# A decoder layer in one launch: the last self-attention batch reordered, and the last two routed tiles given other buffers

## The reference

```
x = layernorm(x + self_attention(x))      # 16 heads of 64, w_qkv 256x3072, w_out 1024x256, bias
x = layernorm(x + cross_attention(x, ctx))# 16 heads of 16, 375 keys, mask, four 256x256 weights
x = layernorm(x + moe(x))                 # top-1 of 8 experts (silu(gate)*up, down; hidden 512) + shared expert
```

## Time and profile before

| | us |
|---|---|
| median of 3 runs (lowest, highest) | 426.57 (425.27, 428.22) |
| the profiled execution's own time | 427.74 |
| its span | 426.0 |
| mean granted TensorE clock, share of full | 0.988 |

### The profile page before, as it was taken

One profiled execution on the slowest core, in us unless ns is written; L12 is line 12 of the kernel. 1 busy time (PEld: TensorE's weight loads), 2 busy tenths in 40 slices (PEclk: granted clock), 3 DMA queues, 4 the chain that ended last, 5 costly groups with the idle time before them and its releaser, 6 DMA issues.

```text
span 426.0 us, 13100 instructions
## 1 busy us (share of the span) xinstructions
PE 400.1 (94%) x5166; PEld 299.7 (70%) x5167; DVE 253.0 (59%) x729; ACT 208.4 (49%) x603; POOL 50.9 (12%) x79
## 2 busy tenths in 40 slices
PE   8999999999999788999999999999899999999980
PEld 7867877878777565766666666666565476899970
DVE  1367775856757555666667676768673641254432
ACT  1064463343625526687666666667683104344420
POOL 4010000101011001000001010100100054223223
PEclk9999999999999899999999999999999999999996
DMA  8999000000000014050404040920000013222211
GB/s 265 367 382 270 14 2 3 3 4 2 4 3 2 4 38 148 2 187 2 187 0 185 16 171 2 390 95 2 0 4 2 2 62 100 62 62 70 61 34 34
DMA packets 15257, 34.49 MB, mean 81 GB/s; under 512 B 2382, under 2 KB 9151, under 8 KB 13921
## 3 DMA queue, kind: packets, MB, share of 16 engines
q1 hardware_dynamic: 13952, 30.72, 20.5%
q0 software_dynamic: 1104, 2.76, 1.8%
q10 hardware_dynamic: 144, 0.23, 0.2%
HBM read 27.27 MB, written 6.70 MB: 80 GB/s over the span
## 4 chain that ended last, share of the span: by engine, by line
PE 42%; issue 38%; DVE 9%; POOL 3%; ACT 3%; DMA 3%; POOLq 1%; SPq 0%; DVEq 0%; ACTq 0%
PE banks L445 9%; PE banks L831 5%; PE banks L467 4%; PE banks L522 3%; PE banks L487 3%; PE banks L509 3%; PE banks L902 3%; PE banks L923 2%; PE banks L843 2%; DVE p L1159 2%; ACT p L977 2%; PE banks L912 2%; DMA out_x<-p,ids 2%; DVE pT L1168 1%; DVE nm L1151 1%
## 5 line engine op out<-in xcount | busy, mean ns | idle before, releaser
L1289 DVE CUSTOM_DVE_ANT_0 p<-banks,mask 112x375 f32<-112x375 f32 x128 | 62.6, 543 | 28.2 <-PE banks L634 28.1
L1031 ACT ACTIVATE p<-p,nm 112x375 f32<-112x375 f32 x128 | 73.8, 604 | 5.3 <-DVE nm L1289 5.3
L1038 ACT ACTIVATE pT<-banks 128x336 f32<-128x336 f32 x96 | 42.4, 443 | 42.1 <-PE banks L654 41.8
L977 ACT ACTIVATE p<-banks,nm 128x112 f32<-128x112 f32 x128 | 43.4, 365 | 31.7 <-DVE nm L1151 30.5
L654 PEld LDWEIGHTS banks<-ident,p 112*128 112x128 f32 (+1 forms) x384 | 38.3, 139 | 28.9 <-issue 22.1
L654 PE MATMUL banks<-ident,p 112*128 112x112 f32 (+1 forms) x384 | 53.2, 266 | 2.0 <-DVE nm L1289 1.5
L445 PE MATMUL banks<-x2T,arena 128*128 128x224 f32 x256 | 52.1, 359 | 0.0
L445 PEld LDWEIGHTS banks<-x2T,arena 128*128 128x128 f32 x256 | 48.5, 193 | 1.8 <-ACT arena L967 0.2
L360 POOL TENSOR_TENSOR rstd<-veps,minus_half 128x1 f32<-128x1 f32 x14 | 7.7, 551 | 286.8 <-DVE veps L1183 286.8
L1144 DVE TENSOR_SCALAR arena<-banks 128x448 f32<-128x448 f32 x32 | 19.9, 621 | 28.5 <-PE banks L445 28.4
L467 PE MATMUL banks<-arena,x2T 128*32 128x256 f32 (+1 forms) x512 | 29.9, 381 | 0.9 <-issue 0.5
(11 more groups left out here) (143 smaller groups left out, 589.7 us busy)
## 6 DMA issues: line engine op xcount, KB each, us to landing
arena<-in_ug SPq DMA_DIRECT2D x8, 1024.0 KB, 5.5
arena<-in_dn SPq DMA_DIRECT2D x8, 512.0 KB, 6.4
mid<-in_ctxT SPq DMA_DIRECT2D x8, 375.0 KB, 3.0
slots_s<-blank SPq DMA_DIRECT2D x14, 128.5 KB
arena<-in_wqk SPq DMA_DIRECT2D x7, 256.0 KB, 5.9
slots_x<-blank SPq DMA_DIRECT2D x14, 128.0 KB
p<-slots_s SPq DMA_DIRECT2D x9, 128.5 KB, 2.1
kT<-slots_x SPq DMA_DIRECT2D x9, 128.0 KB, 2.0
```

The costliest lines, as they stand in the source:

```text
L977: e = act.activation(p1[g][:, i, 0:S], PE_S1[g % 2][:, i * 128:i * 128 + S], ACT.Exp, bias=nm1[:, n:n + 1], accum_out=rs1[:, n:n + 1])
L1031: act.activation(p2[i % RING], p2[i % RING], ACT.Exp, bias=nm2[:, i % H:i % H + 1], scale=-1.0).then_inc(exp2, 1)
L1038: act.activation(pT2[:, i % RING], PE_T2[r][:, 0:KT * S].rearrange("p (k n) -> p k n", k=KT), ACT.Copy).then_inc(pt2_act, 1)
L1289: v.tensor_tensor_reduce(p2[i % RING], PE_S2[r][0:S, 0:S2], bias[:], 1.0, 3e38, ALU.add, ALU.min, accum_out=nm2[:, i % H:i % H + 1]).then_ ...
```

## The change

In batch 7 (`OUT_EARLY`) TensorE issues `out1(5)` ahead of `score1(1,7)` instead of behind it, and `value1(0,7)` ahead of `between1(7,5)` (the second key half) instead of behind it. VectorE takes the residual sum of tile 5 (`add_rest`) and `evac_v(2,0)` right behind the last row maxima, `evac_q(0)` ahead of `normalise(3)` instead of behind it, and the moments behind `turn_blocks(3)`, with `ln1_b(5)` directly after them.

In the routed tiles the product of tile 8 goes to `hrT_last`, in the array `mid`, and no longer waits for `down(7)`. Tile 7 takes `ids[1]`, `fin[1]` and a semaphore of its own for its store; tile 8 takes `ids[0]`, `fin[0]` and waits for the stores of tiles 0 to 6. GpSimd's loop ends one tile earlier, the last two tiles are written out. SyncE's last wait is split in two.

```diff
+        OUT_EARLY = (B - 1,)
-            def to_out(t, p):
+            def to_out(t, p, done=stored):
...
-            with g.Fori(0, tiles - 1) as t:
+            with g.Fori(0, tiles - 2) as t:
                 root3(t, 0)
                 to_out(t, 0)
-            root3(tiles - 1, 1)
-            to_out(tiles - 1, 1)
+            root3(tiles - 2, 1)
+            to_out(tiles - 2, 1, stored_other)
+            root3(tiles - 1, 0)
+            to_out(tiles - 1, 0)
...
                 between1(b, 1)
+                if b in OUT_EARLY:
+                    out1(b - 2)
                 score1(1, b)
-                if b >= 2:
+                if b >= 2 and b not in OUT_EARLY:
                     out1(b - 2)
...
                 between1(b, 4)
-                between1(b, 5)
                 if b == B - 1:
                     value1(0, b)
-                if b < 2 or b == B - 1:
+                between1(b, 5)
+                if b < 2 or b in OUT_EARLY:
                     value1(1, b)
...
                 rowmax(3, b)
-                if b < 2:
+                if b in OUT_EARLY:
+                    add_rest(PE_W1[:, 0:C], wout1, xb1, b - 2, b % 2, y1)
+                if b < 2 or b in OUT_EARLY:
                     drain1(b, 0)
                 normalise(2, b)
                 turn_blocks(2, b)
-                if b >= 2:
+                if b >= 2 and b not in OUT_EARLY:
                     ln1_a(b - 2)
                     drain1(b, 0)
                 else:
                     drain1(b, 1)
                 normalise(3, b)
                 turn_blocks(3, b)
+                if b in OUT_EARLY:
+                    moments(b - 2, b % 2, y1, st1, ag1, ve1)
                 if b >= 2:
                     ln1_b(b - 2)
+                if b >= 2 and b not in OUT_EARLY:
                     drain1(b, 1)
...
-            def finish(t, first, p=0):
+            def finish(t, first, p=0, kept=0):
...
                 if not first and p == 0:
-                    v.wait_ge(stored, t * 16)
+                    v.wait_ge(stored, t * 16 - kept)
...
-            product(tiles - 1, False)
-            finish(tiles - 2, False)
-            finish(tiles - 1, False, 1)
+            product(tiles - 1, True, hrT_last)
+            finish(tiles - 2, False, 1)
+            finish(tiles - 1, False, 0, 16)
```

More of the change, by code:

```diff
@@ L177, in build @@
         lgT = mid[:, 0, 0:2 * TILE]
-        hr = mid[:, 0, 0:HID]
+        hrT_last = mid[:, 0, 0:HID].rearrange("p (k n) -> p k n", k=HT)
         hrT = spent[:, 2 * C:2 * C + HID].rearrange("p (k n) -> p k n", k=HT)
@@ L232, in build @@
             sem(n) for n in ("xst_pe", "xst_sb", "gu_pe", "g_sb", "h_sb", "wg_sb", "wu_sb", "yr_pe"))
-        sum3, ids_sb, stats3, aggr3, ve3s, rstd3, done3, stored = (
-            sem(n) for n in ("sum3", "ids_sb", "stats3", "aggr3", "ve3s", "rstd3", "done3", "stored"))
+        sum3, ids_sb, stats3, aggr3, ve3s, rstd3, done3, stored, stored_other = (
+            sem(n) for n in ("sum3", "ids_sb", "stats3", "aggr3", "ve3s", "rstd3", "done3", "stored", "stored_other"))
         PE_S1, PE_J1, PE_U1, PE_W1 = bank[0:2], bank[2:4], bank[4:8], bank[7][:, 256:512]
@@ L324, in _ @@
             load_shared(tiles - 1)
-            sp.wait_ge(stored, tiles * 16)
+            sp.wait_ge(stored, tiles * 16 - 16)
+            sp.wait_ge(stored_other, 16)
             sp.sem_inc(pause, 1)
@@ L414, in to_out @@
                 g.indirect_dma_start(flat, bass.IndirectOffsetOnAxis(ids[:, p:p + 1], 0), fin[p], None,
-                                     bounds_check=T - 1, oob_is_err=False).then_inc(stored, 16)
-            with g.Fori(0, tiles - 1) as t:
+                                     bounds_check=T - 1, oob_is_err=False).then_inc(done, 16)
+            with g.Fori(0, tiles - 2) as t:
                 root3(t, 0)
                 to_out(t, 0)
-            root3(tiles - 1, 1)
-            to_out(tiles - 1, 1)
+            root3(tiles - 2, 1)
+            to_out(tiles - 2, 1, stored_other)
+            root3(tiles - 1, 0)
+            to_out(tiles - 1, 0)
         @block.tensor
@@ L603, in _ @@
                     value1(0, b)
-                if 2 <= b < B - 1:
+                if 2 <= b < B - 1 and b not in OUT_EARLY:
                     value1(1, b)
                 between1(b, 4)
-                between1(b, 5)
                 if b == B - 1:
                     value1(0, b)
-                if b < 2 or b == B - 1:
+                between1(b, 5)
+                if b < 2 or b in OUT_EARLY:
                     value1(1, b)
@@ L914, in up, with down @@
                 mm.then_inc(gu_pe, 1)
-            def down(t, e, first):
+            def down(t, e, first, h=hrT):
                 pe.wait_ge(h_sb, t + 1)
@@ L922, in down @@
                 for m in range(HT):
-                    mm = pe.matmul(YB[:, 0:C], hrT[:, m, :], arena[:, bass.ds(e[m], C)], start=(m == 0), stop=(m == HT - 1))
+                    mm = pe.matmul(YB[:, 0:C], h[:, m, :], arena[:, bass.ds(e[m], C)], start=(m == 0), stop=(m == HT - 1))
                 mm.then_inc(yr_pe, 1)
@@ L957, in _ @@
             d = downs(tiles - 1)
-            down(tiles - 1, d, False)
+            down(tiles - 1, d, False, hrT_last)
         @block.scalar
@@ L1467, in evac_x, with product @@
                 v.tensor_copy(xsT, bank[0][:, 0:KC * 128].rearrange("p (k n) -> p k n", k=KC)).then_inc(xst_sb, 1)
-            def product(t, first):
+            def product(t, first, h=hrT):
                 v.wait_ge(g_sb, t + 1)
@@ L1473, in product @@
                     v.wait_ge(yr_pe, t)
-                v.tensor_tensor(hrT.rearrange("p k n -> p (k n)"), gr[:], bank[4][:], ALU.mult).then_inc(h_sb, 1)
-            def finish(t, first, p=0):
+                v.tensor_tensor(h.rearrange("p k n -> p (k n)"), gr[:], bank[4][:], ALU.mult).then_inc(h_sb, 1)
+            def finish(t, first, p=0, kept=0):
                 v.wait_ge(yr_pe, t + 1)
```

## The result

| | median, us | lowest to highest | runs |
|---|---|---|---|
| kernel before, beside it | 425.99 | 425.27 to 428.22 | 4 |
| changed kernel | 418.93 | 418.82 to 419.62 | 4 |

The ratio is 0.9851, 95% interval 0.9809 to 0.9892: 7.1 us less. Repeated on another occasion it was 419.81 (419.66 to 420.52) against 426.23, ratio 0.9842 (0.9808 to 0.9877). The profiled execution took 418.82 us with a span of 417.1, against 427.74 and 426.0.

The account below looks back on a forecast made before the run. TensorE is busy 94% of the span, so gains must come where it rests or runs slowly. 5.4 + 2.3 = 7.7 off the profiled 427.74 gives 420.0; allowing for a lower median, 419.4 us was predicted, range 417.6 to 422.4.

Parts of the forecast that it names:

- Part one: Batch 7: the new order on TensorE and VectorE ends the stage at 154.4 instead of 159.89, gaining 5.4 us.
- the tail: Routed tiles 6 to 8: tile 8's sum comes at 416.5 instead of 418.83, gaining 2.3 us.
- the dip: Batch 7: TensorE's clock falls to 0.51 after its 3.04 us rest; 1.24 us of the gain hangs on it.
- `out1(5)` into the rest, at full clock, 3.72: Batch 7, TensorE: out1(5) fills the 3.04 us rest and takes 3.72 us, not 5.41; the other end costs 1.7.
- VectorE's chain: Batch 7: maxima, residual sum, evac_v, normalisation, evac_q, second normalisation and transposition, reckoned to end at 153.4.
- The root's wait hidden with a slack of 0.15: VectorE's ln1_b(5) waits for GpSimd's root until 155.35, first maximum due 155.5; costed at nothing, bounded at 0.5.
- Carried through cross-attention: Everything behind batch 7 moves with it; cross-attention starts with the same spacing as before.
- Rival 3: Cross-attention: VectorE late to its maxima gives back half of 5.4, 422.5 to 423.5 us; chance 0.10.
- rival 1: Batch 7 and tail: typical runs lack the clock dip and late store, gain 5.0, time 421.6 us; chance 0.17.
- The home worth nothing: Tail: the last product's own buffer gains 0, VectorE's order holding it; at most 0.69 were the 2.18 absent.
- Tile 6's wait stays: Tail: tile 6's ids keep their 2.18 us wait for a store to land.
- A second HAM failure mode: psum-queue depth-cycling: Batch 7: short rests between matmul groups could swing the clock, losing 1.7 us per further stretch; rival chance 0.04.

Follow-up runs that it names:

- e6_no_swap: Changed kernel with value1(0,7) back behind the second key half; 421.28 us, kernel before beside it 426.73.
- e4_out_early: Kernel before with only out1(5) moved ahead of score1(1,7); 427.08 us, ratio 1.003 to the kernel before.
- f2_before: Kernel before, unaltered, run for a second trace; 424.77 us (one run).
- f3_before: Kernel before, unaltered, run for a third trace; 424.85 us (one run).
- e2_tail: Kernel before with only the tail's part (own home of the last product, exchanged output buffers), batch 7 as before; 424.69 us, ratio 0.9970.
- e5_out_late: Changed kernel with out1(5) back behind score1(1,7); 423.66 us, ratio 0.9945 to the kernel before.
- f1_after: Changed kernel, unaltered, run once more; 419.81 us against 426.23 for the kernel before, ratio 0.9842.
- e7_no_home: Changed kernel with the last product back in the shared buffer hrT, waiting for down(7); 420.11 us, kernel before beside it 426.73.
- e1_batch7: Kernel before with only the new order of batch 7, tail as before; 420.69 us, ratio 0.9869 to the kernel before.

## Why the prediction was right

The forecast of 419.4 (417.6 to 422.4) met 418.93 and 419.81. Part one is right in its mechanism and its size. That the sum lands so close is partly luck: the tail was put at 2.3, which holds for one of its two cases and not the usual one. With the dip and without the late store, which is what the mean clocks and the traces say of a typical run, the parts make 5.70 + 0.7 = 6.4. I had 7.2 against the median of 426.57; the medians beside the changed kernel lay lower, at 425.99 and 426.23. The steps:

- *`out1(5)` into the rest, at full clock, 3.72*: right, 3.62; it began during the transposes. `score1(1,7)` started 5.06 behind `score1(0,7)` (145.16 - 140.10) instead of 4.70 before.
- *VectorE's chain*: right step by step. With the 0.36 of the earlier start taken off, the first scores came 5.70 earlier; I had reckoned 5.4 for the end of `value1`. 0.3 came from the earlier start of `out1(5)`, shorter copies (0.41, 1.23) and handovers.
- *The root's wait hidden with a slack of 0.15*: hidden, slack 0.34.
- *Carried through cross-attention*: right, -0.06 over 251 us. Rival 3 is out.
- *The tail*: the 2.3 were for executions with both waits, and hold between them: T 15.01 in the trace before, 12.67 in e6_no_swap, 2.34. Without the long wait it is 0.7, as rival 1 had it (0.8).
- *The home worth nothing*: right for the profiled execution only. Undisturbed it is 0.46, inside the bound of 0.69 that I kept.
- *Tile 6's wait stays*: wrong for the trace after, where it was absent. There the profiled pair fell by 8.9 and not 7.7.

Where I judged badly is the weight of rival 1, the stalls that typical runs don't have. I set against it that TensorE's rest of 3.04 us is made by dependences. The rest is; the fall of the clock behind it is not in every execution: among six traces with a rest of 2.9 to 3.04 us in batch 7 it fell in two (the first trace before, e4_out_early), and stayed at 1.00 in four (f2_before, f3_before, e2_tail, e5_out_late). The mean clocks correct that picture: 41 of 53 runs before are below 0.994, so the half of rival 1 that has typical runs without the dip is wrong. Its other half holds: the late store of tile 5 held up tile 6's ids for 1.5 to 2.3 us in only four traces of fourteen. An execution before without either gains 4.35 + 0.7 = 5.1, one with both 5.70 + 2.34 = 8.0; the medians moved by 7.1 and 6.4, between these. Rival 1's 421.6 was too late since it started from a median that holds some of these stalls, and took off the gain of an execution without any.

The clock dip agrees in part with the Trainium skill, "TensorE: Matmul & The Clock Gate", section "HAM oscillation — how this bites in real kernels", which has a rest send the clock to half: both dips followed a rest of about 3 us, none came without, but four such rests were followed by none. The section that I had weighed against the change, "A second HAM failure mode: psum-queue depth-cycling", is not borne out here: in the seven traces with `out1(5)` early and VectorE's new order no stretch of batch 7 was below full clock, although the work comes in the same short pieces.

Why tile 5's store lands late in some executions can be read from its packets, as far as traces go. In the trace before, an instruction packet fell into them, and the landing took 4.69 us. In f1_after the same two stand together. DMA queues of f1_after (packets, MB, share of 16 engines' time), 401.5 to 403.5 us:

```profile
q0 software_dynamic: 45, 0.10, 14.8%
q8 instruction: 1, 0.02, 2.9%
```

The store has 48 packets; the last three follow behind, from 403.86 to 405:

```profile
q0 software_dynamic: 3, 0.01, 4.0%
```

In f2_before the store was not late. There all 48 start between 406 and 407.6, and the instruction packet starts only between 407.6 and 407.9:

```profile
q0 software_dynamic: 48, 0.11, 20.0%
...
q8 instruction: 1, 0.02, 29.6%
```

Packet by packet, in us behind the issue of tile 5's store:

| trace | instruction packet | 46th packet of the store starts | its last packet ends |
|---|---|---|---|
| before | 1.86 to 3.52 | 3.51 | 4.22 |
| e7_no_home | 1.84 to 3.34 | 3.33 | 4.04 |
| f1_after | 1.96 to 2.88 | 2.87 | 3.58 |
| e6_no_swap | 2.69 to 3.62 | 3.61 | 4.32 |
| the ten others | ended by 1.05, from 2.38 on, or none near | 2.02 to 2.03 | 2.05 to 2.07 |

In all four late stores three packets are held until the instruction packet is through, and in the ten others the two don't overlap. The Trainium skill, "DMA: Bandwidth & Descriptors", section "Queues, rings and completion order", lets an engine finish one row's packet before it turns to another row's, which would make such a meeting cost time; the four agree with it. It stays a coincidence of times and not an experiment: a kernel that moves the packet away was not tried, and in e6_no_swap the instruction packet starts 0.6 us after the other 45 are through, so that what held the three until then is open.

## What to carry to other kernels

Look for a piece of work that needs nothing of the present batch and put it into the wait that the batch must have, but move its consumer too: early production alone earned 0, early consumption (with the split `value1`) alone 1.45, both 4.35. Before summing a gain from one trace, ask of each stall whether the order makes it or the execution: here the rest was in every trace with the old order, the dip and the late landing were not, and the one trace had both. A figure that every run carries, here the mean clock, says more about how common a stall is than a few traces do. The second output buffer earns less in the usual execution (0.2) than in one with a late store (2.4), since it cuts the chain by which that store delays the next tile.

## What I had not expected of the hardware

- The same rest of TensorE, 3.04 us at the same place of the same program, is followed by some 3.2 us at half clock in one execution and by none in two others. Why it differs is open.
- A single instruction packet of 0.02 MB went with a store that landed up to 2.3 us later (4.79 us in e6_no_swap against 2.47).
- The start of batch 7 varies from 138.2 to 141.3 us between executions, whatever the kernel. One piece of that lies in the first value projection, where TensorE stood still on nothing that the profile shows for 1.72 us in e1_batch7 and not at all in f3_before:

```profile
25.99 2.79 PE L469 MATMUL banks<-arena,x2T 128*32 128x256 f32 x46 [1.72 <-issue]
```

and the row of f3_before:

```profile
22.66 4.27 PE L467 MATMUL banks<-arena,x2T 128*32 128x256 f32 x64
```

Differences of 1 us between single executions of this kernel mean little unless the distances are taken behind this place.
